# Six graph-attention layers in one pipeline: one value projection in five a slot later, mask products apart from layer 0's scores, GpSimd's scale and shift by graph

## The reference

```python
# layer 0: 8 heads of 32
q, k, v = x @ Wq + bq, x @ Wk + bk, x @ Wv + bv          # split into heads
attn = softmax(where(adj == 0, -inf, q @ k.T * scale))   # per head
y = (attn @ v) @ Wo + bo + x
x = layer_norm(y) * gamma + beta
# layer 1: one head, width 256: the same, with out @ Wo + bo + x
# layers 2 to 5: one head; q, k are 128 wide, with biases; v is x itself
scores = where(adj == 0, -1e10, q @ k.T / sqrt(128))
ctx = (where(adj == 0, 0, softmax(scores)) @ x) @ Wc.T
x = layer_norm(x + ctx) * gamma + beta
```

## Time and profile before

| | us |
|---|---|
| median of 3 runs | 2556.24 (2555.07 to 2557.42) |
| the profiled execution | 2563.42 |
| its span, first to last instruction | 2561.6 |
| TensorE busy | 2378.7 |
| GpSimd busy | 1862.4 |
| VectorE busy | 1782.8 |
| ScalarE busy | 1593.2 |
| mean granted clock of TensorE | 0.984 |

### The profile page before, as it was taken

One profiled execution on the slowest core, in us unless ns is written; L12 is line 12 of the kernel. 1 busy time (PEld: TensorE's weight loads), 2 busy tenths in 40 slices (PEclk: granted clock), 3 DMA queues, 4 the chain that ended last, 5 costly groups with the idle time before them and its releaser, 6 DMA issues.

```text
span 2561.6 us, 57112 instructions
## 1 busy us (share of the span) xinstructions
PE 2378.7 (93%) x20944; PEld 2201.7 (86%) x20944; DVE 1782.8 (70%) x4874; ACT 1593.2 (62%) x5512; POOL 1862.4 (73%) x2439
## 2 busy tenths in 40 slices
PE   5899999999999999999999999999999999999995
PEld 4788898898898898898888898898898898898884
DVE  2567767777767767767777777777767777767773
ACT  4566666666666666666666666666666666666652
POOL 3577777777777777777777777778777778777773
PEclk8999999999999999999999999999999999999997
DMA  3000000000000000000000000000000000000000
GB/s 139 22 22 22 28 26 22 28 26 22 28 26 22 28 26 22 28 26 22 28 26 22 28 26 22 28 26 22 28 26 20 30 26 22 28 26 16 14 9 13
DMA packets 38150, 68.62 MB, mean 27 GB/s; under 512 B 4336, under 2 KB 12656, under 8 KB 37232
## 3 DMA queue, kind: packets, MB, share of 16 engines
q1 hardware_dynamic: 37872, 64.97, 7.5%
HBM read 48.18 MB, written 16.78 MB: 25 GB/s over the span
## 4 chain that ended last, share of the span: by engine, by line
PE 78%; POOL 11%; DVE 8%; issue 1%; ACT 1%; DMA 0%; POOLq 0%; SPq 0%; DVEq 0%
PE qk_bank L373 15%; PE value_bank L382 15%; PE context_bank L523 9%; PE unit_bank L373 7%; PE qk_bank L478 5%; PE unit_bank L435 4%; PE unit_bank L456 4%; PE unit_bank L382 3%; PE score_bank L507 3%; POOL x_out L919 3%; POOL x_out L921 3%; PE unit_bank L425 3%; PE unit_bank L447 2%; DVE y L796 2%; PE score_bank L514 2%; PE score_bank L504 2%
## 5 line engine op out<-in xcount | busy, mean ns | idle before, releaser
L815 DVE TENSOR_SCALAR y<-y,mv,rstd 128x256 f32<-128x256 f32 x768 | 513.9, 710 | 298.8 <-POOL rstd L900 298.8
L373 PE MATMUL qk_bank<-xT_hi,w_lo 128*128 128x256 f32 x1280 | 406.1, 317 | 121.6 <-DVE xT_lo L761 121.6
L619 ACT CAST xT_hi<-qk_bank 128x512 fp32r<-128x512 f32 x320 | 189.9, 594 | 455.4 <-PE qk_bank L478 455.4
L919 POOL TENSOR_TENSOR x<-y,rows 128x512 f32<-128x512 f32 x320 | 407.8, 1274 | 88.5 <-DVE y L815 85.3
L921 POOL TENSOR_TENSOR x<-x,rows 128x512 f32<-128x512 f32 x320 | 411.7, 1287 | 25.1
L599 ACT ACTIVATE probs<-unit_bank,negmax 128x128 f32<-128x128 f32 x1024 | 365.4, 379 | 60.4 <-DVE negmax L733 60.4
L373 PEld LDWEIGHTS qk_bank<-xT_hi,w_lo 128*128 128x128 f32 x1280 | 242.7, 190 | 178.2 <-DVE xT_lo L761 172.7
L382 PE MATMUL value_bank<-w_lo,xT_hi 128*128 128x256 f32 x1280 | 393.3, 307 | 0.0
L905 POOL TENSOR_TENSOR probs<-probs,rtotal 128x256 f32<-128x256 f32 x512 | 318.2, 643 | 74.5 <-DVE rtotal L746 74.5
L382 PE MATMUL value_bank<-w_hi,xT_lo 128*128 128x256 f32 x1280 | 366.3, 286 | 0.0
L382 PE MATMUL value_bank<-w_hi,xT_hi 128*128 128x256 f32 x1280 | 365.8, 286 | 0.0
(11 more groups left out here) (89 smaller groups left out, 6469.0 us busy)
## 6 DMA issues: line engine op xcount, KB each, us to landing
x0T<-xT_in SPq DMA_DIRECT2D x64, 256.0 KB, 2.6
x<-x_in SPq DMA_DIRECT2D x64, 256.0 KB, 2.7
out<-x_out SPq DMA_DIRECT2D x64, 256.0 KB, 2.1
adj<-adj_in SPq DMA_DIRECT2D x64, 128.0 KB, 2.2
rows<-rows_in SPq DMA_DIRECT2D x1, 1920.0 KB, 11.6
probs0T<-w_in SPq DMA_DIRECT2D x1, 1024.0 KB, 4.9
probs<-w_in SPq DMA_DIRECT2D x1, 1024.0 KB, 8.0
x<-w_in SPq DMA_DIRECT2D x1, 1024.0 KB, 14.0
```

The lines of the kernel that those rows point to most:

```text
L373: mm = pe.matmul(psum[:, n * G * N:(n + 1) * G * N], split(w, name, kd, at, at + P), flat(xT_half[:, kd]), start=kd == 0 and w is w_lo, st ...
L815: m = dve.tensor_scalar(y[:, r, g], y[:, r, g], mv[:, r, g, 0:1], rstd[:, r, g:g + 1], ALU.subtract, ALU.mult)
L919: pool.tensor_tensor(new, y[:, r], row_of_each(f"gamma{layer}"), ALU.mult).then_inc(zg_ready, 1)
```

## The change

Three things are changed.

- `project_v(i)` of items with i % 5 == 4 (all of layer 2) is no longer issued in slot i but in slot i+1, right behind `score(i)`. ScalarE's `move_v` of these items goes behind `softmax` in that slot instead of ahead of it.
- `score0` is cut in two: `open_scores0` with all the waits and the four mask products stays where `score0` was, and the 32 small products follow behind `project_qk(i)`.
- `scale_and_shift` on GpSimd multiplies one graph at a time and adds one graph at a time, four instructions of 128x256 in place of two of 128x512; VectorE's `normalise` signals after each graph, and the counts in the waits follow.

```diff
+def late_values(i):
+    return i % PERIOD == STEP
...
-            def score0(group):
+            def open_scores0(group):
...
                 for j in range(QUAD):
                     pe.matmul(unit_bank[j][:, :], eye16[:, :],
                               mask[:, group % HELD].unsqueeze(2).to_broadcast([P, G, QUADS, N]),
                               start=True, stop=False)
+
+            def score0(group):
                 for g in range(G):
...
                 if item(i - 1):
                     score(i - 1)
+                if item(i - 1) and late_values(i - 1):
+                    project_v(i - 1)
                 if (group := due(i, 6)) is not None:
-                    score0(group)
+                    open_scores0(group)
...
                 if item(i):
                     project_qk(i)
+                if (group := due(i, 6)) is not None:
+                    score0(group)
...
-                if item(i):
+                if item(i) and not late_values(i):
                     project_v(i)
...
-                if item(i - 1) and item(i - 1)[0] != 1:
+                if item(i - 1) and item(i - 1)[0] != 1 and not late_values(i - 1):
                     move_v(i - 1)
...
                 if item(i - 1):
                     softmax(i - 1)
+                if item(i - 1) and late_values(i - 1):
+                    move_v(i - 1)
                 if (group := due(i, 6)) is not None:
                     exp0(group, 0)
...
                 for g in range(G):
-                    m = dve.tensor_scalar(y[:, r, g], y[:, r, g], mv[:, r, g, 0:1], rstd[:, r, g:g + 1],
-                                          ALU.subtract, ALU.mult)
-                m.then_inc(z_ready, 1)
+                    dve.tensor_scalar(y[:, r, g], y[:, r, g], mv[:, r, g, 0:1], rstd[:, r, g:g + 1],
+                                      ALU.subtract, ALU.mult).then_inc(z_ready, 1)
...
-                pool.wait_ge(z_ready, NORM_AT[norm] + 1)
-                pool.tensor_tensor(new, y[:, r], row_of_each(f"gamma{layer}"), ALU.mult).then_inc(zg_ready, 1)
-                pool.wait_ge(zg_ready, AFFINE_AT[norm] + 1)
-                pool.tensor_tensor(new, new, row_of_each(f"beta{layer}"), ALU.add).then_inc(x_ready, 1)
+                for g in range(G):
+                    pool.wait_ge(z_ready, G * NORM_AT[norm] + g + 1)
+                    pool.tensor_tensor(new[:, g], y[:, r, g], row(f"gamma{layer}"), ALU.mult).then_inc(zg_ready, 1)
+                for g in range(G):
+                    pool.wait_ge(zg_ready, G * AFFINE_AT[norm] + g + 1)
+                    m = pool.tensor_tensor(new[:, g], new[:, g], row(f"beta{layer}"), ALU.add)
+                m.then_inc(x_ready, 1)
```

More of the change, by code:

```diff
@@ L262, in split, with row @@
             return which[:, at + kd * width + lo:at + kd * width + (width if hi is None else hi)]
+        def row(name):
+            return rows[:, ROWS.index(name), :]
         def row_of_each(name):
@@ L793, in add_residual @@
                 if at >= YS:
-                    dve.wait_ge(zg_ready, AFFINE_AT[NORMS[at - YS]] + 1)
+                    dve.wait_ge(zg_ready, G * (AFFINE_AT[NORMS[at - YS]] + 1))
                 for g in range(G):
```

## The result

The changed kernel takes 2788.72 us (median of 4 runs, 2786.76 to 2789.78) against 2556.83 for the kernel before: a ratio of 1.0906, interval 1.0887 to 1.0924. It is slower by 231.9 us, which is 3.74 for each of the 62 rounds. The ratios are of undisturbed executions; one of 8256 us, among ten near 2552 of the run called "the postponement alone", is left out of its ratio.

The account below looks back on a forecast made before the run. TensorE, busy 93% of the span, was taken as the bound, through its work and the holes in its stream. 62 x 2.36 = 146, + 44 - 14 for the clock, gave +176: 2732 us, range 2668 to 2808.

Parts of the forecast that it names:

- Part 2: Scores behind the projection: `transpose_x` waits 2.9 us for `move_qk` behind `exp0`, in the slot holding layer 0's scores.
- the hole of r4: In the slot holding layer 0's scores, TensorE's `project_qk` waits 0.8 us for `xT_lo`.
- TensorE's lateness at r0's projection: In the slot behind layer 0's scores, TensorE wants `project_qk` 1.85 us later than before.
- Part 1: Values one slot later: the move costs nothing and alone swallows at best 1.5 us of a 1.9 us hole.
- Part 3: GpSimd by graph: about 0.25 us saved per norm, 0.5 for two; `normalise` about 1.32 us instead of 2.70.
- A pair of halves takes 1.15: GpSimd's 128x256 products: two pairs take 2.3 us per norm, where whole products take 2.58.
- That half of the step which concerned `normalise`: VectorE beside GpSimd's 128x256 products: `normalise` takes about 1.32 us instead of 2.70.
- The clock: The clock falls in 37 of 62 rounds at a price of 1.2 us each, adding 44 us.
- GpSimd's 0.5: GpSimd's late transposed units of `probs0`: the last 0.5 us of the round's growth of 2.36.
- the old falls: Nine clock falls already in the kernel before, 1.56 us each: 14 us taken off the sum.
- the clock falls in every round: Rival: the clock falls each round, 62 x (2.36 + 1.56) - 14 = +229, 2785 us; chance 0.15.
- What the new profile was to show: `move_qk` waits of 2.9 us, 62 times, as largest; `probs` waits 0.1 to 0.4; slow clock in half the rounds.

Follow-up runs that it names:

- the postponement alone: Kernel before, with only GpSimd's last-layer scale and shift one slot later and ScalarE unchanged: 2552.75 us against 2558.39, ratio 0.9978.
- both remedies: Changed kernel plus 20 unread matmuls in the hole before `transpose_x`, and VectorE's first row maxima moved behind `add_residual` and `statistics`: 2674.11 us, ratio 1.0445.
- the square of four runs: Changed kernel 2789 us; with VectorE's first row maxima behind the statistics (GpSimd in time) 2788; with 20 unread matmuls (clock held) 2741; with the two together 2674.
- ScalarE's order alone: Changed kernel with ScalarE's `move_qk` and `move_probsT` ahead of `exp0(group, 0)`, VectorE as in the change: 2746.92 us against 2558.39, ratio 1.0732.
- both orders changed: Changed kernel with ScalarE's `move_qk` and `move_probsT` ahead of `exp0(group, 0)`, and VectorE's row maxima behind the statistics: 2610.44 us, ratio 1.0194.
- part 2 alone: Kernel before, with only the 32 small score products moved behind the projection: 2731.08 us against 2557.25, ratio 1.0688.
- part 3 alone: Kernel before, with only GpSimd's scale and shift done by graph: 2563.54 us against 2557.25, ratio 1.0025.

## Why the prediction came out as it did

**Part 2, the step on which all hung, was right.** The chain of scores, row maxima, `exp0` and `move_qk` was put at a hole of 2.9 us and measured 2.80, the hole of r4 at 0.8 and measured 0.64. With the clock held and GpSimd in time the round grows by 1.91 us (40.19 against 38.28), where the working gave 1.85 for TensorE's lateness at r0's projection. That the place of `exp0` is the cause is shown by the run that changed only the orders of the queues.

**Part 1 was right.** By itself it was said to cost nothing and to swallow at best part of the hole; the run gave 0.9985 and two holes.

**Part 3 was wrong in sign.** "A pair of halves takes 1.15" took the price of `probs0`, products of the same size. The scale and shift by graph takes 2.76 to 2.85 per norm (1426.45 to 1429.30 for the longer), against 2.58 whole and 2.3 forecast. That half of the step which concerned `normalise` held: 1.54 against 1.32 expected. The page "GPSIMD Engine Reference" of the Trainium skill, section "3.1 Elementwise — side-by-side cycle accounting", sets a dispatch cost against every instruction, and the prediction set it aside. Here two more instructions cost 0.18 to 0.27 us per norm, in the direction of that rule; that `probs0` shows no such cost stays unexplained. A candidate not tried is its second operand, which is one value spread over a row.

**The clock was the mis-sized term.** The prediction took 37 of 62 rounds at 1.2 us, 44 us. The clock fell in all of them, in a third for about twice as long. A round has a mean of 42.04 us where it is 40.19 with both remedies, which is 1.85 for the clock in each. With GpSimd in time, the clock alone makes 114 us (2788 against 2674). The forecast also put the clock's price on top of GpSimd's 0.5 and subtracted only 0.35; the square of four runs shows that GpSimd's lateness, 67 us by itself, is hidden altogether once the clock falls. The two errors had opposite signs: the clock was 70 too low, and 62 x 0.51 = 32 us for GpSimd should not have been added. That they partly cancel is luck, and it leaves 38 of the 57 by which 2732 missed.

Most of the rest lies in the sum without these two. The kernel with both remedies is 117 us over the one before, and the forecast has 62 x 1.85 less 14 for the old falls, 101. The 1.91 explains 4 of the 16; the remainder stays open. One candidate is that the 9 old falls were counted in the profiled execution, which is 7 us slower than the median they were taken off.

The rival "the clock falls in every round" gave 2785. It kept GpSimd's 0.51, which was not to be seen, and charged 1.56 for a fall where the mean was 1.85, so it too came close partly by luck.

**What the new profile was to show** it showed in the main: the wait for `move_qk` as TensorE's largest, `normalise` shorter, r0's hole gone. The slow level was to be in half of the rounds and was in all. TensorE's wait for `probs` did not appear, for the reason above, until the clock was held.

## What to carry to other kernels

Before moving work on the engine that sets the time, follow its result through every queue that reads it: here 1.1 us of matmuls moved behind 1.6 us of others put 2.4 us of ScalarE's queue in front of an instruction that the same TensorE needed next. A hole in TensorE's stream costs more than its length where the clock falls behind it, and then hides other lateness, so remedies must be tried together. Look first for work that nobody waits for (here the last layer's output) in the crowded stretch of a side engine, and move it to where that engine idles: together with two exponentials put later and two more buffers it gave 3.4%.

## What the runs showed of the hardware

- After a hole of 2.8 us in each round the granted clock fell to 1.2 GHz in every one of 57 rounds; after one of 2.35 (ScalarE's order alone) in 28 of 57; after one of 1.76 in 9 of 57; after one of 1.52 (both orders changed) in none of 57; and after a pair of 1.37 and 2.07, with 2 us of work between, in 3 of 52. The last is rarer than after 1.76 alone, though 2.07 is the longer hole, so the length of one hole may not decide alone. Where the falls are few they are evenly spaced: with part 2 alone they come at 458, 1198 and 1939 us, 18 rounds apart. Twenty matmuls that nobody needs, put in the hole of 2.8, made the kernel 48 us faster.
- VectorE's `normalise` (two instructions, float32, 128x256) took 0.74 us with GpSimd all but idle, 1.32 beside two products of 128x256 (`probs0`), 1.54 beside two by graph, 2.70 beside two of 128x512. The last three pairs end 0.14 to 0.15 us behind the end of GpSimd's second product (1273.78 behind 1273.64, 1279.97 behind 1279.82, 1428.06 behind 1427.91). So VectorE was held up by whole instructions of GpSimd, and not slowed in one proportion. The page "Advanced Engine Details and Errata" of the Trainium skill, section "VectorE Performance Modes", says that the second SBUF port of VectorE is shared with GpSimd, and that GpSimd's instructions and VectorE's two-port instructions interfere with or block each other. The four numbers agree with it; that these instructions use both ports is not shown.
- A GpSimd product of two tensors took 748 ns by graph at 128x256 (part 3 alone) and 1274 at 128x512 (the kernel before). If the rest goes by size, some 0.2 us of each is fixed (2 x 748 - 1274 = 222). The `probs0` products speak against a fixed part common to all: at 640 ns two of them cost no more than one of 128x512.
